# A turn's steps in another order: inverse, third norm and feed-forward part between the operator's product and the attention that uses it

## The chip, the cores and the metric

One core of a Trainium2 chip runs the whole program. The metric is the device time of one execution in microseconds (us), as the median of several runs. The core has five engines that each work through their own list of instructions in order: TensorE (PE, with its weight loads shown apart as PEld), VectorE (DVE), ScalarE (ACT), GpSimd (POOL) and SyncE (SP), which here only issues DMAs. They wait for each other by semaphores.

## What is computed

The input is 4 x 1024 rows of 256. A chunk is 128 rows, so there are 32 chunks, 8 to a batch. Cut to what matters:

```python
x = x + attn(layernorm(x))            # attn has a norm and a residual of its own
x = x + ffn(layernorm(x))             # "third norm"

def attn(x):                          # per head (16) and chunk (128 rows)
    G = K.T @ K + eps * I;  W = solve(G, K.T @ V)
    U = I[:, :8]
    for _ in range(2): U, _ = qr(W @ U)
    S = 0.9 * S + U @ (U.T @ W)       # state, carried from chunk to chunk of a batch
    out = 0.125 * (Q @ S)             # then @ Wo, + x

def ffn(x):                           # 256 -> 1024 -> 256, weights binarized
    h = gelu(x @ bw1.T + b1)
    return h @ bw2.T + b2
```

## The kernel before

Everything runs in float32, but for the feed-forward part, whose activations are split into a high and a low float16 half (`y3t`, `hsplit`). The first part of the program projects keys and values (L1286), forms the Gram products (L1332), inverts blocks of them by sweeps on DVE ("pivots", L1136, L1142, L1148), and works out low-rank factors per chunk, which go through DRAM (`f_d`). The queries are never formed: the factors of all heads of a chunk give one 256 x 256 operator.

The second part is 32 **turns**, one for each chunk. A turn has these steps:

- LF: SP loads the chunk's factors into `fl` (three buffers), after AU of three turns before was filled. LR: SP loads the residual rows, after the attention sum of two turns before.
- NB `apply_inverse` (PE, 8 matmuls, L1497), copied by ACT (L987) to `nb` (two buffers).
- AU `operator` (PE, 4 matmuls, L1504). DVE `decay` (L1204, L1201 on a batch's first chunk) adds it to 0.9 times the state before and writes one of two `state` buffers.
- AT `attend` (PE, 4 matmuls, L1511), which reads that state. DVE `attention_out` (L1213 to L1219) makes the residual sum `x2`, its statistics and the variance. POOL raises the variance to the power -1/2 (L781) and adds the output bias to `x2` (`biased`, L751).
- X3 `third_norm` (DVE, L1225) writes `x3`. Y3 `turn` (PE, 2 transpositions, L1519); ACT writes the high half of `y3t` (L993), DVE the low half (L1232).
- HID `hidden` (PE, 32 matmuls, L1531). GE0 and GE1, the two halves of `gelu` (ACT, 4 activations at L1002 and a cast at L1007 each). LO0 and LO1, `low` (POOL, L759), the low halves of the hidden values. LO1 waits for the cast of GE1.
- OUT `output` (PE, 16 matmuls, L1541), finished by DVE (L1238, L1241) and stored by SP.

The order is written by a planner, `plan()`, which runs on the host when the program is built. It has streams of steps (projections, Schur steps, solves, `tail`, and `turn`) and a simple clock for each engine with weights per step (`PE_WEIGHT`, `ACT_WEIGHT`, `DVE_WEIGHT`, `POOL_WEIGHT`). It takes the next step of a stream that can start, gives it a PSUM bank or two of the eight, and puts it into one list, `ORDER`. The stream `turn` comes last, so turns fill PE where the others can't. Within a stream the order is fixed. Every engine then walks through the same `ORDER` and does its own part of each step: `for step, c in ORDER:`. So the order of the steps of a turn is the order in PE's queue, in ACT's, in DVE's, in POOL's and in SP's. Two of these lists matter most here. POOL does its part of AT (L781, L751) and of LO0 and LO1 where these stand in the list; ACT does its part of Y3 (L993) and of GE0 and GE1 where these stand.

The tuple at L257 gives the order of a turn. Iteration r holds steps of several turns, r-2 to r+4. The pivots (step PIV) and the inverses of small blocks (SML) are put on DVE between the others, when the planner's clock of DVE says that it is free. POOL's MB (`block_small`, L742) spreads a batch's small inverses; for batches 2 and 3 it waits until the last NB of two batches before was filled.

Of the kernel before, what the change touches and what calls it, by code (L numbers as in the profile page):

```python
# [16 lines left out]
CPB = SEQ // CHUNK  # L17
# [23 lines left out]
             NB=1, AU=1, AT=1, Y3=1, HID=2, OUT=1)  # L41
# [1 line left out]
                 W=1.1, Y=.8, YT=.45, Z=.75, ZT=.5, BQ=1.87, BO=1.87, NB=.57, AU=.95, AT=.95, Y3=.35, HID=1.87, OUT=1.85)  # L43
ACT_WEIGHT = dict(T=.95, KL=.65, LG=.35, KC=.65, KT=.65, KA=.65, KB=.65, VA=.65, VB=.65, G=1.35, FT=1.1, FB=.4, QT=.65, SP=.65, SX=2.4, SV=.95, S=.45, U=2.1,
                  W=1.2, Y=.9, YT=1.0, Z=.45, ZT=.55, BQ=.65, BO=.65, NB=.45, Y3=.45, GE0=2.2, GE1=2.2)
DVE_WEIGHT = dict(AU=.75, AT=1.4, X3=.45, Y3=.5, OUT=.95)
POOL_WEIGHT = dict(LO0=1.25, LO1=1.25)

SMALL = ("SP", "SX", "SV", "S", "U", "W", "Y", "YT", "Z", "ZT", "NB", "Y3")
# [15 lines left out]
def pivot_weight(t):  # L65
    return .65 + .00204 * HALF * (HALF - 1 - t)


def plan():
# [4 lines left out]
    order, where, before = [], {}, {}  # L74
# [3 lines left out]
    now = dict(pe=0.0, act=0.0, dve=5.0, pool=5.0)  # L78
# [9 lines left out]
    def advance_dve():  # L88
        while True:
            while norms and now["dve"] <= now["pe"] + 4.0:  # L90
                g = norms[0]
                behind = FIRST[g] < sum(1 for c in range(NCH) if ("T", c) in where) + 4
                if staged and staged[0][1] <= now["dve"] + 1.0 and not behind:
                    break
                norms.pop(0)
                order.append(("LN", g))
                now["dve"] = max(now["dve"], now["pe"] - 2.0) + LN_WEIGHT * GROUPS[g] + .6
                for c in range(FIRST[g], FIRST[g] + GROUPS[g]):
                    at["LN", c] = now["dve"]
            for b, t in list(small_at.items()):  # L100
                if t <= now["pe"]:
                    del small_at[b]
                    order.append(("SML", b))
                    order.append(("MSTORE", b))
                    now["dve"] = max(now["dve"], t) + 8.0
                    spread_at[b] = now["dve"] + 3.0
            for b, t in list(spread_at.items()):
                if t <= now["pe"]:
                    del spread_at[b]
                    order.append(("MI", b))  # L110
                    mask_at[b] = now["pe"] + 4.0
            for b, t in list(mask_at.items()):
                if t <= now["pe"]:
                    del mask_at[b]
                    order.append(("MB", b))
                    small_done[b] = now["pe"] + 3.0
            ripe = [s for s in waiting if open_at.get(s, 1e9) <= now["pe"]]
            if ripe and len(staged) < 2:
                s = min(ripe, key=lambda s: s[1] + 1.5 * s[0])
                waiting.remove(s)  # L120
                sweep_order.append(s)
                j = len(sweep_order) - 1
                order.append(("SLOAD", j))
                staged.append((j, now["pe"] + 10.5))
                pivots[j] = 0
            if not staged:
                now["dve"] = max(now["dve"], now["pe"])
                return
            j, loaded = staged[0]
            start = max(now["dve"], loaded)  # L130
            if start > now["pe"] + DVE_BEHIND:
                return
            t = pivots[j]
            order.append(("PIV", (j, t)))
            now["dve"] = start + pivot_weight(t)
            pivots[j] += 1
            if pivots[j] == HALF:
                now["dve"] += .6
                order.append(("SSTORE", j))
                staged.pop(0)  # L140
                which, b = sweep_order[j]
                at["swept", which, b] = now["dve"] + 6.0
                if which == 0:
                    waiting.append((1, b))
# [31 lines left out]
    def put(step, c):  # L176
        order.append((step, c))
        if step in BANKS:
# [8 lines left out]
            if step in ACT_WEIGHT:  # L187
                now["act"] = max(now["act"], now["pe"] + .15) + ACT_WEIGHT[step]
                end = now["act"] + .15
                if step in DVE_WEIGHT:  # L190
                    now["dve"] = max(now["dve"], end) + DVE_WEIGHT[step]
                    end = now["dve"] + .15
            elif step == "HID":
                end = 1e9
            else:
                now["dve"] = max(now["dve"], now["pe"] + .15) + DVE_WEIGHT[step]
                end = now["dve"] + .15
# [8 lines left out]
        elif step == "X3":  # L206
            now["dve"] = max(now["dve"], at["AT", c] + 1.5) + DVE_WEIGHT[step]
            at[step, c] = now["dve"] + .1
# [11 lines left out]
        elif step == "BO" and c % half_batch == half_batch - 1:  # L220
            order.append(("MLOAD", c // half_batch))
            small_at[c // half_batch] = at["Z", c] + 7.0
        advance_dve()
        for b in small_done:
            at["small", b] = small_done[b]
# [28 lines left out]

    turn = []
    for r in range(-4, turns + 3):
        for step, n in (("LF", r + 4), ("LO1", r - 1), ("AT", r + 1), ("LR", r + 3), ("OUT", r - 2), ("X3", r + 1), ("NB", r + 2),  # L257
                        ("HID", r), ("GE0", r), ("AU", r + 2), ("LO0", r), ("Y3", r + 1), ("GE1", r)):
            if 0 <= n < turns:
                turn.append((step, n))  # L260

# [16 lines left out]
    def pause():  # L278
        now["pe"] += .25
        advance_dve()  # L280
        for b in small_done:
            at["small", b] = small_done[b]
# [17 lines left out]


ORDER, SWEEPS, WHERE, BEFORE = plan()


# [1323 lines left out]
```

## Time and profile before

| | us |
|---|---|
| median of 3 runs | 900.69 |
| lowest and highest | 897.38, 904.1 |
| the profiled execution | 900.93 |
| its span, first to last instruction | 899.1 |

| engine | busy us | share of the span |
|---|---|---|
| PE | 783.1 | 87% |
| PEld | 530.6 | 59% |
| DVE | 631.7 | 70% |
| ACT | 490.1 | 55% |
| POOL | 227.4 | 25% |

The profiled execution took 1.8 us more than its span. The rows of the trace below give the start of an instruction from the span's start, its duration, the engine and line, and in brackets how long the engine had been idle before it and what released it. Several instructions of one line in a row are merged into one row: its duration then runs from the first start to the last end.

### The profile page before, as it was taken

How to read it: one execution, taken by the hardware profiler on the slowest of the kernel's cores; microseconds unless marked ns; L12 is line 12 of the kernel's file. 1: busy time of each engine (PE TensorE's matmuls, PEld its weight loads, DVE VectorE, ACT ScalarE, POOL GpSimd, SP SyncE). 2: the span in 40 equal slices, each digit the busy share in tenths (PEclk: the TensorE clock that was granted, in tenths of full speed). 3: DMA queues.
4: the chain of work that ended last, by engine and by line, in shares of the span. 5: the costliest groups of instructions: out<-in, count | busy, mean ns of one | idle time of the engine just before them, and what ended most of it. 6: DMA issues, size and time to landing. Idle time of an engine off the chain costs nothing.

```text
span 899.1 us, 34359 instructions
## 1 busy us (share of the span) xinstructions
PE 783.1 (87%) x14730; PEld 530.6 (59%) x14730; DVE 631.7 (70%) x1336; ACT 490.1 (55%) x1068; POOL 227.4 (25%) x297
## 2 busy tenths in 40 slices
PE   4999999999999998988687687888798888899996
PEld 2555555565555555656455565666576666677775
DVE  3666399089998999980798988889953304666664
ACT  1864444555455454554444465556566665466665
POOL 4666100201001100000201012652012203555554
PEclk9999999999999999999879888999999999899999
DMA  8555211653455636655734645344456432222210
GB/s 313 155 159 167 77 62 42 205 177 122 139 162 160 185 72 168 185 162 168 162 79 119 188 116 159 103 135 116 107 154 138 104 93 69 62 82 74 77 43 30
DMA packets 174662, 114.43 MB, mean 127 GB/s; under 512 B 134128, under 2 KB 152944, under 8 KB 173488
## 3 DMA queue, kind: packets, MB, share of 16 engines
q1 hardware_dynamic: 168784, 91.00, 36.8%
q0 software_dynamic: 5728, 21.24, 7.5%
q8 instruction: 117, 1.92, 0.9%
q14 instruction: 33, 0.27, 0.1%
HBM read 61.22 MB, written 50.99 MB: 125 GB/s over the span
## 4 chain that ended last, share of the span: by engine, by line
PE 66%; DVE 13%; issue 9%; DMA 5%; ACT 4%; SPq 1%; POOL 1%; POOLq 0%; DVEq 0%; ACTq 0%
PE psum L1286 25%; PE psum L1332 6%; PE psum L1531 6%; PE psum L1541 5%; DVE outer L1142 4%; PE psum L1473 3%; PE psum L1511 3%; DVE work L1148 3%; PE psum L1504 2%; PE psum L1388 2%; PE psum L1375 2%; PE psum L1362 2%; PE psum L1423 2%; DVE state L1204 2%; PE psum L1497 1%
## 5 line engine op out<-in xcount | busy, mean ns | idle before, releaser
L1286 PE MATMUL psum<-wkv,xhat 128*128 128x512 f32 x512 | 240.3, 613 | 4.3 <-ACT xhat L834 4.3
L1142 DVE SCALAR_TENSOR_TENSOR outer<-work,rd 128x992 f32<-128x992 f32 (+30 forms) x248 | 189.6, 764 | 8.9 <-DVE rd L1136 0.3
L1148 DVE TENSOR_TENSOR work<-work,outer 128x992 f32<-128x992 f32 (+30 forms) x248 | 176.3, 711 | 8.6
L1286 PEld LDWEIGHTS psum<-wkv,xhat 128*128 128x128 f32 x512 | 93.2, 192 | 105.3 <-issue 99.5
L871 ACT COPY kv<-psum 128x512 f32<-128x512 f32 x128 | 75.1, 587 | 120.8 <-PE psum L1286 120.5
L1002 ACT ACTIVATE late<-psum,b1c,alpha 128x128 f32<-128x128 f32 x256 | 96.7, 461 | 49.6 <-PE psum L1531 49.6
L759 POOL TENSOR_TENSOR hsplit<-late,hsplit 128x512 f16<-128x512 f32 x64 | 77.4, 1211 | 142.4 <-ACT hsplit L1007 142.3
L1531 PEld LDWEIGHTS psum<-y3t,s1t 128*128 128x128 f16 x1024 | 61.3, 102 | 17.7 <-issue 16.7
L1531 PE MATMUL psum<-y3t,s1t 128*128 128x128 f16 x1024 | 66.9, 227 | 4.4 <-DVE y3t L1232 4.0
L1541 PE MATMUL psum<-s2t,hsplit 128*128 128x256 f16 x512 | 63.7, 279 | 4.0 <-POOL hsplit L759 2.7
L1332 PE MATMUL psum<-kv 128*64 128x128 f32 x1024 | 64.4, 280 | 0.0
L1541 PEld LDWEIGHTS psum<-s2t,hsplit 128*128 128x128 f16 x512 | 50.5, 100 | 15.6 <-issue 4.6
L1332 PEld LDWEIGHTS psum<-kv 128*64 128x64 f32 x1024 | 56.6, 139 | 4.9 <-issue 4.3
L1511 PE MATMUL psum<-state,xhat 128*128 128x256 f32 x128 | 39.4, 435 | 22.4 <-DVE state L1204 17.8
L1204 DVE SCALAR_TENSOR_TENSOR state<-state,psum 128x512 f32<-128x512 f32 x28 | 19.2, 686 | 42.3 <-PE psum L1504 42.3
L1133 DVE TENSOR_SCALAR work<-work 128x32 f32<-128x32 f32 x8 | 1.5, 192 | 65.7 <-DMA work<-lead_in_d 65.7
L1136 DVE RECIPROCAL rd<-work 128x1 f32<-128x1 f32 x256 | 41.7, 163 | 8.0
L1423 PE MATMUL psum<-cu,rr 64*64 64x64 f32 x1024 | 35.4, 230 | 8.9 <-issue 6.4
L1007 ACT CAST hsplit<-late 128x512 f16<-128x512 f32 x64 | 39.5, 618 | 5.9 <-ACT late L1002 0.7
L1511 PEld LDWEIGHTS psum<-state,xhat 128*128 128x128 f32 x128 | 24.2, 210 | 30.4 <-issue 25.0
L927 ACT COPY cu<-psum 32x1024 f32<-32x1024 f32 x32 | 32.1, 1005 | 17.5 <-PE psum L1410 17.3
L981 ACT COPY late<-psum 128x512 f32<-128x512 f32 x32 | 18.8, 586 | 40.4 <-PE psum L1473 40.0
(130 smaller groups left out, 1279.5 us busy)
## 6 DMA issues: line engine op xcount, KB each, us to landing
gc_d<-gc SPq DMA_DIRECT2D x32, 384.0 KB, 2.5
schur_mem<-gc_d SPq DMA_DIRECT2D x32, 384.0 KB, 4.2
f_d<-late SPq DMA_DIRECT2D x16, 512.0 KB, 3.6
late<-f_d SPq DMA_DIRECT2D x32, 256.0 KB, 2.7
sv_d<-sv SPq DMA_DIRECT2D x16, 384.0 KB, 3.1
lead_d<-work POOLq DMA_DIRECT2D x4, 1024.0 KB, 5.0
schur_mem<-lead_d SPq DMA_DIRECT2D x32, 128.0 KB, 4.3
r_d<-pt SPq DMA_DIRECT2D x16, 256.0 KB, 2.2
```

The costliest lines, as they stand in the source:

```text
L759: nc.gpsimd.tensor_tensor(hsplit[:, r % 2, 1, t].rearrange("p t r -> p (t r)"), ht[:, BANK * n:BANK * (n + 1)], hsplit[:, r % 2, 0, t].rea ...
L871: nc.scalar.copy(kv[:, n, BANK * half:BANK * (half + 1)], place(step, c)).then_inc(drain(step, c), 1)
L1002: nc.scalar.activation(ht[:, P * t:P * (t + 1)], place("HID", r)[:, P * t:P * (t + 1)], ACT.Gelu, scale=alpha1[:, t:t + 1], bias=b1c[:, t: ...
L1136: V.reciprocal(rd[:, t:t + 1], a[:, t, t:t + 1]).then_inc(swept, 1)
L1142: V.scalar_tensor_tensor(out=tile, in0=a[:, t, t + 1:HALF].unsqueeze(2).broadcast_to([P, m, HALF]), scalar=rd[:, t:t + 1], in1=a[:, t, t + ...
L1148: V.tensor_tensor(rest, rest, tile, ALU.subtract).then_inc(swept, 1)
L1286: ins = mm(dst[:], xnt[:, c, t], wkv[:, n, t, BANK * half:BANK * (half + 1)], start=t == 0, stop=t == KT - 1)
L1332: ins = mm(dst[side(a), P * h:P * (h + 1)], kv[:, 0, cols], kv[:, :, cols], start=True, stop=True)
L1423: ins = mm(dst[side(a ^ n), at:at + HD], u if turned else r, r if turned else u, start=True, stop=True)
L1511: ins = mm(dst[:, 0:DM], xnt[:, TURNS[r], t], state[:, r % 2, DM * t:DM * (t + 1)], start=t == 0, stop=t == KT - 1)
L1531: ins = mm(dst[:, P * t:P * (t + 1)], s1t[:, k, P * t:P * (t + 1)], y3t[:, part, k], start=k + part == 0, stop=k + part == KT)
L1541: ins = mm(dst[:, 0:DM], hsplit[:, r % 2, part, t], s2t[:, t], start=t + part == 0, stop=t + part == FT)
```

## The change

In `plan()` the steps of iteration r are put into another order, NB runs one turn further ahead, two weights of DVE are raised, and MB is placed only when the NB that it waits for stands in the list.

```diff
-DVE_WEIGHT = dict(AU=.75, AT=1.4, X3=.45, Y3=.5, OUT=.95)
+DVE_WEIGHT = dict(AU=.75, AT=1.4, X3=.8, Y3=.5, OUT=1.45)
...
             for b, t in list(mask_at.items()):
-                if t <= now["pe"]:
+                if t <= now["pe"] and (b < 2 or ("NB", CPB * (b - 1) - 1) in where):
                     del mask_at[b]
                     order.append(("MB", b))
...
     turn = []
     for r in range(-4, turns + 3):
-        for step, n in (("LF", r + 4), ("LO1", r - 1), ("AT", r + 1), ("LR", r + 3), ("OUT", r - 2), ("X3", r + 1), ("NB", r + 2),
-                        ("HID", r), ("GE0", r), ("AU", r + 2), ("LO0", r), ("Y3", r + 1), ("GE1", r)):
+        for step, n in (("LF", r + 4), ("LO1", r - 1), ("AT", r + 1), ("LR", r + 3), ("OUT", r - 2), ("AU", r + 2), ("NB", r + 3),
+                        ("X3", r + 1), ("HID", r), ("Y3", r + 1), ("GE0", r), ("LO0", r), ("GE1", r)):
             if 0 <= n < turns:
                 turn.append((step, n))
```

By engine, iteration r reads:

| engine | before | after |
|---|---|---|
| PE | AT(r+1) OUT(r-2) NB(r+2) HID(r) AU(r+2) Y3(r+1) | AT(r+1) OUT(r-2) AU(r+2) NB(r+3) HID(r) Y3(r+1) |
| DVE | AT(r+1) OUT(r-2) X3(r+1) AU(r+2) Y3(r+1) | AT(r+1) OUT(r-2) AU(r+2) X3(r+1) Y3(r+1) |
| ACT | NB(r+2) GE0(r) Y3(r+1) GE1(r) | NB(r+3) Y3(r+1) GE0(r) GE1(r) |
| POOL | LO1(r-1) AT(r+1) LO0(r) | LO1(r-1) AT(r+1) LO0(r) |
| SP | LF(r+4) LR(r+3) OUT(r-2) | LF(r+4) LR(r+3) OUT(r-2) |

The instructions themselves are the same in number and shape.

## Rows read from the trace of the kernel before

**Rows 1.** Busy time by stretch: bounds, length, engines, granted clock, DMA share, GB/s.

```profile
550.00:600.00 50.00, 40.49 (x532) 31.10 (x530) 41.20 (x97) 27.24 (x65) 27.62 (x33) 0.90 0.34 100
800.00:850.00 50.00, 45.44 (x465) 35.84 (x464) 31.70 (x64) 33.90 (x87) 25.90 (x28) 1.00 0.26 75
```

**Rows 2.** Groups by line: names, shapes, count; busy us, mean ns; idle before, releasers.

```profile
L1511 PE MATMUL psum<-state,xhat 128*128 128x256 f32 x128 | 39.4, 435 | 22.4 <-DVE state L1204 17.8 <-DVE state L1201 4.6
```

**Rows 3.** Timeline, PE alone, one turn of the last stretch.

```profile
822.28 1.10 PE L1511 MATMUL psum<-state,xhat 128*128 128x256 f32 x4 [0.65 <-DVE state L1204]
823.22 1.91 PE L1541 MATMUL psum<-s2t,hsplit 128*128 128x256 f16 x16
825.05 0.63 PE L1497 MATMUL psum<-late,mblock 32*32 32x256 f32 x8
825.62 1.96 PE L1531 MATMUL psum<-y3t,s1t 128*128 128x128 f16 x32
827.42 1.08 PE L1504 MATMUL psum<-late 128*128 128x256 f32 x4
828.34 0.38 PE L1519 MATMUL psum<-ident,x 128*128 128x128 f32 x2
829.38 1.10 PE L1511 MATMUL psum<-state,xhat 128*128 128x256 f32 x4 [0.66 <-DVE state L1201]
```

**Rows 4.** Timeline, the other engines in the same turn.

```profile
822.64 0.36 ACT L993 CAST y3t<-psum 128x256 f16<-128x256 f32 x1
...
822.91 1.51 ACT L1002 ACTIVATE late<-psum,b1c,alpha 128x128 f32<-128x128 f32 x4
...
825.20 1.16 POOL L759 TENSOR_TENSOR hsplit<-late,hsplit 128x512 f16<-128x512 f32 x1 [1.23 <-ACT hsplit L1007]
...
825.62 1.02 DVE L1241 TENSOR_TENSOR yo<-yo,x2b 128x256 f32<-128x256 f32 x1
...
826.32 0.73 POOL L781 TENSOR_TENSOR rs<-ve,half_neg 128x1 f32<-128x1 f32 x1
...
827.09 0.81 DVE L1225 TENSOR_SCALAR x<-x,mv,rs 128x256 f32<-128x256 f32 x1 [0.44 <-POOL rs L781]
...
828.54 0.69 DVE L1201 COPY state<-psum 128x512 f32<-128x512 f32 x1 [0.64 <-PE psum L1504]
```

**Rows 5.** Timeline, all engines, the last turns up to the end.

```profile
878.01 0.38 PE L1519 MATMUL psum<-ident,x 128*128 128x128 f32 x2
...
883.85 0.81 DVE L1225 TENSOR_SCALAR x<-x,mv,rs 128x256 f32<-128x256 f32 x1 [0.44 <-POOL rs L781]
...
884.80 0.41 PE L1519 MATMUL psum<-ident,x 128*128 128x128 f32 x2 [1.12 <-DVE x L1225]
...
888.80 1.51 ACT L1002 ACTIVATE late<-psum,b1c,alpha 128x128 f32<-128x128 f32 x4 [0.48 <-PE psum L1531]
...
890.92 1.50 ACT L1002 ACTIVATE late<-psum,b1c,alpha 128x128 f32<-128x128 f32 x4
...
893.20 1.15 POOL L759 TENSOR_TENSOR hsplit<-late,hsplit 128x512 f16<-128x512 f32 x1 [0.96 <-ACT hsplit L1007]
```

**Rows 6.** Timeline, three turns among pivots of DVE, and POOL's power there.

```profile
573.22 0.57 POOL L781 TENSOR_TENSOR rs<-ve,half_neg 128x1 f32<-128x1 f32 x1
...
584.74 1.10 PE L1511 MATMUL psum<-state,xhat 128*128 128x256 f32 x4 [1.69 <-DVE state L1204]
...
594.07 1.76 PE L1511 MATMUL psum<-state,xhat 128*128 128x256 f32 x4 [2.88 <-DVE state L1204]
...
602.84 1.10 PE L1511 MATMUL psum<-state,xhat 128*128 128x256 f32 x4 [0.66 <-DVE state L1201]
```

**Rows 7.** Timeline, two waits of PE outside these stretches.

```profile
488.95 2.05 PE L1511 MATMUL psum<-state,xhat 128*128 128x256 f32 x4 [2.80 <-DVE state L1201]
...
766.35 3.57 PE L1531 MATMUL psum<-y3t,s1t 128*128 128x128 f16 x32 [4.01 <-DVE y3t L1232]
```

**Rows 8.** DMA issues of the page: engine, count, KB each, us to landing.

```profile
late<-f_d SPq DMA_DIRECT2D x32, 256.0 KB, 2.7
```

## The prediction, as written before the changed kernel was run

> **What bounds the kernel now.** I read the busy times first, by stretch. In the last stretch, where nothing is left but turns, PE is busy 45.4 of 50 us at a granted clock of 1.00, and no other engine passes 36 [rows 1]. So a turn is worth what PE's queue takes for it, waits included. The groups by line then say where PE stands still in a turn: before AT it was idle for 22.4 us in all, and what ended that was DVE's `decay` [rows 2]. PE alone in one turn shows the pattern [rows 3]: from one AT to the next 7.10 us, of which 0.66 is that wait. The work is thus 6.44 us: by the starts AT 0.94, OUT 1.83, NB 0.57, HID 1.80, AU 0.92, Y3 0.38. The wait has its cause in the order: AU is followed by Y3 alone (0.38), while the decay that AT needs starts 1.12 after AU's start and takes 0.69 [rows 3, 4]. From 772.6 to 879.1 us sixteen ATs follow each other like this, 7.10 apart, all but one behind a wait of 0.64 to 0.66.
>
> **The change part by part.**
>
> *AU goes ahead of NB and HID.* Between AU(r+2) and the AT(r+2) that needs it now stand NB, HID and Y3: 0.57 + 1.80 + 0.38 = 2.75 us of PE's work, against 1.12 + 0.69 = 1.81 less AU's own 0.92. The wait before AT goes. Taken alone that is 0.66 of each turn, and 22.4 us of the span at the most [rows 2].
>
> *What comes late next.* The third norm needs POOL's power (L781), and POOL, in order, comes to it only after LO1(r-1), which stands ahead of AT(r+1) in the list. LO1(r-1) waits for the cast of GE1(r-1). That was so before. What is new is ACT's order: Y3(r) now stands ahead of both GE0(r-1) and GE1(r-1), before it stood between them. So each Y3 holds back the whole gelu of a turn, that gelu holds back LO1, LO1 the power, and the power the next Y3. This closes a ring from Y3 to the next Y3, and its length, worked out from rows:
>
> - Y3 start on PE to the high half on ACT: 0.42 (its own 0.38, and 0.04 as from AU's 827.42 + 1.08 to the decay at 828.54 [rows 3, 4]).
> - high half to GE0: 822.91 - 822.64 = 0.27 [rows 4].
> - GE0 to GE1: 890.92 - 888.80 = 2.12 [rows 5].
> - GE1 to LO1: 825.20 - 822.91 = 2.29 [rows 4].
> - LO1 to the power: 826.32 - 825.20 = 1.12 [rows 4].
> - the power to X3: 827.09 - 826.32 = 0.77 in this turn. The power took 0.73 there, beside DVE's `yo` sum of 1.02, and 0.57 in another turn [rows 4, 6]. With X3 waiting, nothing runs on DVE then, so I take 0.57 + 0.04 = 0.61.
> - X3 to Y3: 884.80 - 883.85 = 0.95 [rows 5].
>
> The sum is 7.78 us, or 7.94 with the slower power. In the order before, the ring ran from Y3 over GE1 alone: 7.78 - 2.12 = 5.66, shorter than the turn of 7.10, and PE never waited for it, except where it shows itself once: with AU and NB used up, the last Y3 came 1.12 late, behind X3 [rows 5].
>
> The Trainium skill, page "GPSIMD Engine Reference", section "1. Specifications", says that GpSimd's access to SBUF is shared with VectorE and contended by a DVE instruction with two SBUF inputs. The pair of 0.73 and 0.57 agrees. By it the ring would be 7.78 if the `yo` sum has ended by then, and 7.94 if not; it should have ended some 2 us before.
>
> A turn therefore costs max(6.44, 7.78) = 7.78, 0.68 more than before: the wait moves from AT (0.66) to Y3 (7.78 - 6.44 = 1.34).
>
> *How many turns.* From Y3(15) at about 771.5 to Y3(30) at 878.0 are 15 intervals, and one more to Y3(31): 16 x 0.68 = 10.9 us. Behind Y3(31) come 0.42 + 0.27 + 2.12 to GE1(30), 2.22 to GE0(31) (a gelu half with its cast: 822.91 plus 2.29, less the 0.07 to LO1), 2.12 to GE1(31), 2.29 to LO1(31), and then 899.12 - 893.20 = 5.92 to the end [rows 5], 15.36 in all. Before, the end came 899.12 - 878.01 = 21.11 after Y3(30) [rows 5]; now 7.78 + 15.36 = 23.14, so 2.0 more, of which 0.68 is counted. The sum is 10.9 + 1.3 = +12.2.
>
> *Turns among pivots.* Around 565 to 603 us PE has turns only, while DVE works on pivots. Their ATs waited up to 2.88, and the two intervals from 584.74 to 602.84 took 9.05 each, one of them with AT at 1.76 instead of 1.10, a spell at the lower clock behind the long wait [rows 6]. Bounds: if the waits go and nothing comes, the two turns fall to 7.78, 2.5 us less, and all five turns there lose some 3 to 5; if a pivot of over 2 us stands in front of X3, in the ring, they stay at 9 or pass it. I take -1.
>
> *Turns among other work.* There the turns are 12 to 48 us apart, the ring is no bound, and waits before AT go: 2.80 at 488.95 [rows 7], and four of 0.50 to 0.70. Against it stands that ACT, in order, now sits before Y3's high half with GE0 and every copy behind it. Bounds -5 and +3; I take -3. The 4.01 at 766.35 [rows 7], behind DVE's small inverse, I leave: HID waits for `y3t` in either order, only which turn it hits changes.
>
> *NB a turn further ahead.* It needs `fl` a turn earlier. The load lands 2.7 us after its issue [rows 8]; SP comes to it in iteration r-1 behind the store of OUT, and NB of that chunk is on PE in iteration r+1, so some 8 us of PE's work still cover it. If that cover were gone, 2.7 a turn at most. LF and LR stay where they were on SP, behind the same waits. The copy of NB on ACT (0.37) falls behind GE1 and has a turn until its AU. Nothing.
>
> *AU ahead of X3 on DVE.* The decay (0.69) ends 1.12 + 0.69 after AU's start, 0.38 + 0.94 + 1.83 + 1.81 = 4.96 us after the last Y3; X3 can start only 6.8 after it. Hidden, unless the ring were shorter than I say; then it is the next bound.
>
> *MB and the weights.* MB(2) and MB(3) already stand behind NB(7) and NB(15). Nothing. The larger weights move pivots a little; no more than the bounds above.
>
> Together 12.2 - 1 - 3 = +8.2: the profiled execution from 900.9 to 909.1, its span from 899.1 to 907.3. The median lies 0.2 under the profiled execution, so 908.9.
>
> **The rivals.**
>
> *The ring is hidden, the waits simply go* (faster). If the high half got to ACT without holding the gelu, or X3 were no longer behind LO1, each of 16 turns would fall to 6.44: -10.6, with the mixed part -4 to -8 more: 882 to 886. It decides the sign from a ring under 7.10. For it speaks only that PE has 0.66 to give back. Against it that each of the seven links has its row, and queues of ACT and POOL are in order.
>
> *The gains among other work are larger* (within 1%). The five waits there all go (-5), and the turns among pivots come down by 5 with the spell at the lower clock gone: 12.2 - 10 = +2.2, 903.
>
> *The mixed part loses too.* Pivots fall into the ring in five turns, at 1 to 2 us each, and Y3 waits now and then elsewhere: 12.2 + 5 to 10, 918 to 923.
>
> *PE's clock falls in the last stretch.* Now a wait of 1.34 us stands in each turn. A wait of 1.69 was followed by an AT of 1.10, at full clock, one of 2.88 by 1.76 [rows 6], and HID behind 4.01 took 3.57 instead of 1.96 [rows 3, 7]. So 1.34 should keep the 2.4 GHz. At 1.2 GHz, by the ratios 1.76/1.10 and 3.57/1.96, 6.44 would be some 11 us: if a fifth of the last sixteen turns went so, 3 x 3.2 = +10, 919. The Trainium skill, page "TensorE: Matmul & The Clock Gate", section "A second HAM failure mode: psum-queue depth-cycling", tells of a kernel whose frequent small pauses between groups of matmuls make the clock swing; the granted 1.00 over waits of 0.65 in each turn [rows 1, 3] does not bear that out here, and no row has 1.34 in each turn.
>
> **How the numbers follow.** The forecast's case (905 to 913) 0.46, larger gains 0.22, losses in the mixed part 0.15, the clock 0.08, the hidden ring 0.09. The range leaves out the hidden ring and the far end of the losses: 899 to 920. About 1% is what a measurement of this kernel can tell from no change; that is 891.7 to 909.7. Faster has the hidden ring, 0.08. The forecast's case lies on the upper edge: a little over half of it, with the larger gains, is within 1%, so 0.48; the rest is slower, 0.44.
>
> **What would show it.** In the changed kernel's last stretch: Y3 to Y3 at 7.8 us, no wait before L1511, one of 1.3 before L1519 released by DVE's `x` (L1225), X3 released by POOL's power, the power straight behind L759, L993 just ahead of L1002. Wrong if Y3 has no wait there, if the turn is 6.5, or if 7.8 holds and the total still falls: then the mixed part gave back more than 12.

## The result, and the profile after

| | before | after |
|---|---|---|
| median, us | 899.04 (4 runs) | 921.91 (4 runs) |
| lowest to highest | 893.63 to 904.1 | 916.88 to 927.04 |
| profiled execution, its span | 900.93, 899.1 | 916.88, 915.0 |

The ratio is 1.0256 (95% interval 1.0162 to 1.035). Six more runs on another chip, beside new ones of before, give 1.027 (1.0194 to 1.0345). The change makes the kernel some 2.6% slower. I had forecast 908.9 (899 to 920), 8.2 us more than before, and it is 22.9: the right side, much too small, and outside the range. The profiled execution, 916.88, is the fastest of the four.

PE does the same work in less of a longer span. Its waits by group of instructions (busy us, mean ns, idle before):

```profile
L1511 PE MATMUL psum<-state,xhat 128*128 128x256 f32 x128 | 36.0, 407 | 0.0
L1519 PE MATMUL psum<-ident,x 128*128 128x128 f32 x64 | 14.1, 305 | 44.2 <-DVE x L1225 44.1
L1531 PE MATMUL psum<-y3t,s1t 128*128 128x128 f16 x1024 | 64.5, 222 | 10.2 <-DVE y3t L1232 9.3 <-issue 0.6 <-ACT hsplit L1007 0.3
```

The 22.4 us before AT [rows 2] are gone to the last tenth, and 44.2 stand before Y3, where there were 1.4. The kernel before:

```profile
L1519 PE MATMUL psum<-ident,x 128*128 128x128 f32 x64 | 13.0, 287 | 1.4 <-DVE x L1225 1.1 <-ACT wmem L936 0.2
```

One turn of the last stretch of the changed kernel, all engines, in order of time:

```profile
803.36 1.16 POOL L759 TENSOR_TENSOR hsplit<-late,hsplit 128x512 f16<-128x512 f32 x1 [0.96 <-ACT hsplit L1007]
804.48 0.55 POOL L781 TENSOR_TENSOR rs<-ve,half_neg 128x1 f32<-128x1 f32 x1
...
805.07 0.80 DVE L1225 TENSOR_SCALAR x<-x,mv,rs 128x256 f32<-128x256 f32 x1 [1.78 <-POOL rs L781]
806.01 0.41 PE L1519 MATMUL psum<-ident,x 128*128 128x128 f32 x2 [1.43 <-DVE x L1225]
806.26 1.03 PE L1511 MATMUL psum<-state,xhat 128*128 128x256 f32 x4
806.46 0.37 ACT L993 CAST y3t<-psum 128x256 f16<-128x256 f32 x1 [2.90 <-PE psum L1519]
806.73 1.51 ACT L1002 ACTIVATE late<-psum,b1c,alpha 128x128 f32<-128x128 f32 x4
...
808.86 1.50 ACT L1002 ACTIVATE late<-psum,b1c,alpha 128x128 f32<-128x128 f32 x4
...
811.14 1.16 POOL L759 TENSOR_TENSOR hsplit<-late,hsplit 128x512 f16<-128x512 f32 x1 [0.96 <-ACT hsplit L1007]
812.25 0.55 POOL L781 TENSOR_TENSOR rs<-ve,half_neg 128x1 f32<-128x1 f32 x1
...
812.84 0.81 DVE L1225 TENSOR_SCALAR x<-x,mv,rs 128x256 f32<-128x256 f32 x1 [1.78 <-POOL rs L781]
813.79 0.41 PE L1519 MATMUL psum<-ident,x 128*128 128x128 f32 x2 [1.43 <-DVE x L1225]
```

This is the ring as the prediction has it. From Y3 at 806.01: 0.45 to the high half, 0.27 to GE0, 2.13 to GE1, 2.28 to LO1, 1.11 to the power, 0.59 to X3, 0.95 to the next Y3 at 813.79. The sum is 7.78 us. PE waits 1.43 in each turn, for X3; X3 waits for the power.

The busy times by stretch, with the granted clock as the third number from the end, are:

```profile
550.00:600.00 50.00, 35.81 (x858) 28.28 (x858) 38.06 (x78) 26.68 (x60) 22.36 (x25) 0.83 0.49 108
800.00:850.00 50.00, 41.42 (x433) 32.68 (x431) 28.93 (x60) 31.39 (x81) 22.20 (x25) 1.00 0.23 67
```

Against [rows 1] PE has lost 4.7 and 4.0 us of 50; the clock is 0.83 instead of 0.90 in the first and still 1.00 in the second, with a wait of 1.43 in every turn. The first stretch holds other steps in the two kernels (858 matmuls here, 532 before), so that only the second compares like with like. The long waits of PE in the first part all have DVE's queue behind them:

```profile
549.25 0.17 DVE L1164 RECIPROCAL mrd<-msw 128x1 f32<-128x1 f32 x1 [8.21 <-DMA msw<-m_d]
...
556.35 0.41 DVE L1232 TENSOR_TENSOR y3t<-psum,y3t 128x256 f16<-128x256 f32 x1
...
556.91 3.57 PE L1531 MATMUL psum<-y3t,s1t 128*128 128x128 f16 x32 [9.29 <-DVE y3t L1232]
...
570.21 0.20 DVE L1133 TENSOR_SCALAR work<-work 128x32 f32<-128x32 f32 x1 [4.37 <-DMA work<-sv_d]
...
573.04 0.41 DVE L1225 TENSOR_SCALAR x<-x,mv,rs 128x256 f32<-128x256 f32 x1
...
573.59 0.66 PE L1519 MATMUL psum<-ident,x 128*128 128x128 f32 x2 [4.97 <-DVE x L1225]
...
735.63 0.66 PE L1519 MATMUL psum<-ident,x 128*128 128x128 f32 x2 [7.55 <-DVE x L1225]
```

At 549 DVE, in order, sits 8.2 us on a load for the inverse of small blocks (SML), with the low half of Y3(0) behind it, and HID(0) waits 9.29; the HID then takes 3.57 instead of 1.96, and the granted clock from 556 to 561 us is 0.50. At 570 it is a sweep's load and first pivot ahead of X3. At 735 it is SML again, whose small operations hold DVE from 724.3 to 733.8.

**Where the 15.9 us of the two profiled executions lie.** In the changed kernel the other work ends at about 720, with Y3(9) at 721.8; before, at 755, with Y3(14) at 757.9. So five turns fewer had been done by then, and five more stand in the last stretch. Before, Y3(14) to Y3(31) took 884.8 - 757.9 = 126.9; after, Y3(9) to Y3(31) took 899.5 - 721.8 = 177.7, less five turns of 7.10 is 142.2: +15.3. The end behind Y3(31) is 15.5 instead of 14.3: +1.2. What is left, -0.6, is the part among other work. This is a sum for two single executions: that of before was 2 us over its median, that of after 5 under.

### The profile page after: what moved, and what is told of

Same layout as the page of the kernel before. It is cut to its first block, busy times and chain, and to the rows that moved or that the text cites. A ratio compares the mean times of both kernels' runs of the same rounds, so it can differ in the third digit from the quotient of the medians.

```text
span 915.0 us, 34354 instructions
## 1 busy us (share of the span) xinstructions
PE 781.8 (85%) x14730; PEld 529.7 (58%) x14730; DVE 627.2 (69%) x1336; ACT 487.5 (53%) x1068; POOL 225.6 (25%) x297
## 4 chain that ended last, share of the span: by engine, by line
PE 45%; DVE 22%; issue 9%; ACT 9%; POOL 7%; DMA 5%; SPq 2%; POOLq 0%; ACTq 0%; DVEq 0%
PE psum L1286 24%; DVE outer L1142 8%; DVE work L1148 6%; PE psum L1332 6%; POOL hsplit L759 5%; ACT late L1002 4%; DVE x L1225 2%; PE psum L1473 2%; PE psum L1388 2%; DVE rd L1136 2%; ACT hsplit L1007 2%; PE psum L1375 2%; PE psum L1362 2%; PE psum L1423 1%; POOL rs L781 1%
## 5 line engine op out<-in xcount | busy, mean ns | idle before, releaser
L1142 DVE SCALAR_TENSOR_TENSOR outer<-work,rd 128x992 f32<-128x992 f32 (+30 forms) x248 | 186.8, 753 | 8.9 <-DVE rd L1136 0.3
L1148 DVE TENSOR_TENSOR work<-work,outer 128x992 f32<-128x992 f32 (+30 forms) x248 | 172.9, 697 | 8.5
L759 POOL TENSOR_TENSOR hsplit<-late,hsplit 128x512 f16<-128x512 f32 x64 | 75.0, 1172 | 156.6 <-ACT hsplit L1007 156.5
L1002 ACT ACTIVATE late<-psum,b1c,alpha 128x128 f32<-128x128 f32 x256 | 96.5, 460 | 0.0
L1531 PE MATMUL psum<-y3t,s1t 128*128 128x128 f16 x1024 | 64.5, 222 | 10.2 <-DVE y3t L1232 9.3
L1531 PEld LDWEIGHTS psum<-y3t,s1t 128*128 128x128 f16 x1024 | 59.1, 99 | 22.7 <-issue 11.5
L993 ACT CAST y3t<-psum 128x256 f16<-128x256 f32 x32 | 12.0, 374 | 90.0 <-PE psum L1519 89.9
L1232 DVE TENSOR_TENSOR y3t<-psum,y3t 128x256 f16<-128x256 f32 x32 | 13.6, 423 | 63.0 <-ACT y3t L993 63.0
L1519 PE MATMUL psum<-ident,x 128*128 128x128 f32 x64 | 14.1, 305 | 44.2 <-DVE x L1225 44.1
L1225 DVE TENSOR_SCALAR x<-x,mv,rs 128x256 f32<-128x256 f32 x32 | 23.4, 731 | 37.0 <-POOL rs L781 36.9
```

The costliest lines, as they stand in the source:

```text
L759: nc.gpsimd.tensor_tensor(hsplit[:, r % 2, 1, t].rearrange("p t r -> p (t r)"), ht[:, BANK * n:BANK * (n + 1)], hsplit[:, r % 2, 0, t].rea ...
L1002: nc.scalar.activation(ht[:, P * t:P * (t + 1)], place("HID", r)[:, P * t:P * (t + 1)], ACT.Gelu, scale=alpha1[:, t:t + 1], bias=b1c[:, t: ...
L1142: V.scalar_tensor_tensor(out=tile, in0=a[:, t, t + 1:HALF].unsqueeze(2).broadcast_to([P, m, HALF]), scalar=rd[:, t:t + 1], in1=a[:, t, t + ...
L1148: V.tensor_tensor(rest, rest, tile, ALU.subtract).then_inc(swept, 1)
L1531: ins = mm(dst[:, P * t:P * (t + 1)], s1t[:, k, P * t:P * (t + 1)], y3t[:, part, k], start=k + part == 0, stop=k + part == KT)
```

## The experiments

Each ran beside the kernel before. Ratios are to it, with their 95% intervals; "turn" is the time from turn to turn in the last stretch of the profile. Letters are those of the sections below.

| run | what | ratio | turn, us |
|---|---|---|---|
| changed, again | (A) | 1.027 (1.019 to 1.035) | 7.78 |
| gelu_first | (B) GE0 ahead of Y3 | 1.0108 (1.006 to 1.0157) | 6.97 |
| power_first | (B) power ahead of LO1 | 0.9872 (0.9828 to 0.9917) | 6.16 |
| power_only | (B) the same on the old order | 1.0049 (1.0014 to 1.0083) | 7.10 |
| bias_first | (B) ring lengthened | 1.0316 (1.025 to 1.0381) | 8.05 |
| old_then_new | (C) | 1.0108 (1.0055 to 1.0162) | 7.78 |
| new_then_old | (C) | 1.0100 (1.0066 to 1.0134) | 7.10 |
| old_then_power | (C) | 0.9897 (0.9853 to 0.9942) | 6.16 |
| power_from_4 | (C) | 0.9861 (0.9771 to 0.995) | 6.16 |
| weights_only | (D) | 1.0162 (1.011 to 1.0214) | 7.10 |
| old_weights | (D) | 1.0387 (1.0322 to 1.0452) | 7.78 |
| old_weights_power | (D) | 1.0008 (0.9966 to 1.005) | 6.16 |
| small_later | (E) | 1.0291 (1.0246 to 1.0336) | 7.78 |
| small3_later | (E) | 1.023 (1.0173 to 1.0287) | 7.78 |
| small3_power | (E) | 0.9845 (0.9786 to 0.9904) | 6.16 |

**(A) The changed kernel again.**

> The changed kernel once more, beside the next three on one chip, for a narrower interval: 1.020 to 1.030 of before by either theory, the turns of the last stretch at 7.78.

It held: 1.027, 7.78.

**(B) Is it the ring?** Two cuts, at different links:

```diff
 gelu_first:   ... ("X3", r + 1), ("HID", r),
-              ("Y3", r + 1), ("GE0", r), ("LO0", r), ("GE1", r)
+              ("GE0", r), ("LO0", r), ("Y3", r + 1), ("GE1", r)
 power_first:  ("LF", r + 4),
-              ("LO1", r - 1), ("AT", r + 1),
+              ("AT", r + 1), ("LO1", r - 1),
```

> The changed kernel, but with LO1(r-1) behind AT(r+1) in the list, so that POOL does the power and the bias sum of AT before LO1; ACT's order stays that of the change. Theory of the ring: LO1 is no longer in front of the power, the ring is cut at this link, and a turn of the last stretch takes 6.4 to 6.5 us, as with the gelu half moved: span about 886. If ACT's wait for Y3's transposition were itself the price, the turn would stay above 7 us here.

It held for the turn, and went further: 6.16, the span 879.9. That is 19 under the span of before in its one profile, but against the median of before beside this run (895.13, with 885.93 for this kernel) it is only 9 us. Some 20 turns shorter by 0.94 would be 19, so about 10 are lost elsewhere by the medians. PE, POOL and DVE in the last stretch:

```profile
799.69 1.03 PE L1504 MATMUL psum<-late 128*128 128x256 f32 x4
...
800.95 0.73 POOL L781 TENSOR_TENSOR rs<-ve,half_neg 128x1 f32<-128x1 f32 x1
...
801.79 0.73 DVE L1225 TENSOR_SCALAR x<-x,mv,rs 128x256 f32<-128x256 f32 x1
802.34 1.20 POOL L759 TENSOR_TENSOR hsplit<-late,hsplit 128x512 f16<-128x512 f32 x1
803.01 0.39 PE L1519 MATMUL psum<-ident,x 128*128 128x128 f32 x2
803.24 1.03 PE L1511 MATMUL psum<-state,xhat 128*128 128x256 f32 x4
...
804.10 1.91 PE L1541 MATMUL psum<-s2t,hsplit 128*128 128x256 f16 x16
...
805.85 1.03 PE L1504 MATMUL psum<-late 128*128 128x256 f32 x4
```

The power comes before LO1, X3 ends at 802.5, and Y3 at 803.01 has no wait; AU to AU is 6.16. So a turn's work on PE is 6.16 and not the 6.44 that I took as 7.10 less the wait of 0.66. Start to start, 0.81 of the 0.94 lie between Y3 and AT (1.04 before, 0.23 here, for a recorded wait of 0.65), and 0.08 between AT and OUT (0.94 before, 0.86 here). The last 0.05 have nothing to do with the wait: OUT takes 1.83 to 1.84 with NB behind it and 1.75 with AU behind it, and AU takes 0.03 more with NB behind it than with Y3. The rows of the old order in weights_only, at a place with no wait before AT, show the 1.84 all the same:

```profile
784.87 1.03 PE L1511 MATMUL psum<-state,xhat 128*128 128x256 f32 x4
785.74 1.91 PE L1541 MATMUL psum<-s2t,hsplit 128*128 128x256 f16 x16
787.58 0.63 PE L1497 MATMUL psum<-late,mblock 32*32 32x256 f32 x8
```

The wait before AT, recorded as 0.65, had thus cost 0.89 a turn.

> The changed kernel, but with GE0 and LO0 of iteration r put back ahead of Y3(r+1) (as before the change). Theory of the ring: the ring from one Y3 to the next is then 7.78 - 2.12 = 5.66 us, under PE's 6.44 of work, and AU still stands well ahead of AT. So in the last stretch no wait is left before L1511 or L1519, a turn takes 6.4 to 6.5 us, and with some 22 turns there the span falls by 22 x 1.3 = 29 us from 915 to about 886, which is also below the 899 of before. Theory of the planner (the loss comes from where the steps fall among the other work, not from the ring): turns stay near 7.8 or find a new wait, and the span stays above 905.

A miss, in the turn and in the total. The wait of each turn is gone, but one in every second turn has come, and the turns are 6.6 and 7.4 long. The span is 903.0 where 886 was expected, and the ratio 1.0108, though its turns are shorter than the 7.10 of before. The last stretch gives back some 22 x 0.13 = 2.9 us and the end costs 2.0, and the medians are 10 apart, so about 11 us are lost in front of it: in the total the theory of the planner came nearer. PE alone:

```profile
818.08 0.41 PE L1519 MATMUL psum<-ident,x 128*128 128x128 f32 x2 [1.04 <-DVE x L1225]
...
822.57 1.96 PE L1531 MATMUL psum<-y3t,s1t 128*128 128x128 f16 x32
...
824.64 0.41 PE L1519 MATMUL psum<-ident,x 128*128 128x128 f32 x2
...
832.02 0.41 PE L1519 MATMUL psum<-ident,x 128*128 128x128 f32 x2 [1.04 <-DVE x L1225]
```

Two turns take 13.94. There is a second ring, through two turns, which my sum had left out. In the trace of this run it goes from HID(r) at 822.57 to GE0(r) 2.00, to the high half of Y3(r+1) 2.11, to GE1(r) 0.27, to LO1(r) 2.29, to the power 1.25, to X3 0.58, and to Y3(r+2) at 832.02 0.95. From a Y3 that waited (818.08) PE's Y3, AT, OUT, AU and NB take 0.28 + 0.94 + 1.74 + 0.96 + 0.57 = 4.49 to HID. The sum is 13.94, 6.97 a turn, with no slack in it. That this ring sets the pace was not tried by cutting it. If it does, then with POOL's and ACT's old order the hoisted AU could give 7.10 - 6.97 = 0.13 a turn at the most.

```diff
 bias_first, at POOL's part of AT:
+                    biased(c)
                     pool.wait_ge(ve3_ready, c + 1)
                     nc.gpsimd.tensor_tensor(rs3[:], ve3[:], half_neg[:, 0:1], ALU.pow)...
-                    biased(c)
```

> The changed kernel with POOL's two operations of AT swapped: the bias sum (0.72 us) ahead of the power. Theory of the ring: the bias sum comes into the ring (+0.72), and X3, no longer beside it, falls from 0.81 to 0.41 (-0.40): a turn of the last stretch goes from 7.78 to 8.10 us, 22 turns make +7 us against the changed kernel, ratio to before about 1.033. If the wait before Y3 had another cause, the turn stays at 7.78.

It held: 8.05 us for 8.10, and X3 at 0.41 with nothing beside it on POOL. All engines:

```profile
815.95 0.72 POOL L751 TENSOR_TENSOR x2b<-x,b2r 128x256 f32<-128x256 f32 x1
816.63 0.55 POOL L782 TENSOR_TENSOR rs<-ve,half_neg 128x1 f32<-128x1 f32 x1
817.21 0.41 DVE L1225 TENSOR_SCALAR x<-x,mv,rs 128x256 f32<-128x256 f32 x1 [2.46 <-POOL rs L782]
...
817.77 0.41 PE L1519 MATMUL psum<-ident,x 128*128 128x128 f32 x2 [1.71 <-DVE x L1225]
...
825.83 0.41 PE L1519 MATMUL psum<-ident,x 128*128 128x128 f32 x2 [1.71 <-DVE x L1225]
```

`power_only` puts `("AT", r + 1)` ahead of `("LO1", r - 1)` in the kernel before and changes nothing else:

> The kernel before, with one step moved: LO1(r-1) behind AT(r+1), so that POOL does the power ahead of LO1; AU stays where it was. Theory: before the change the power was not late, PE waited for the state; a turn stays at 7.10 and the time does not change (ratio 0.995 to 1.005). If POOL's order were the whole gain of the kernel with LO1 moved, it would show here: a turn near 6.5, ratio below 0.99.

It held: alone, POOL's order gives nothing; by the interval it costs 0.1 to 0.8%. It is worth something only with the wait for the state gone, and of the kernels tried here that hoist AU only those with this swap are faster than before.

**(C) The last stretch and the rest apart.** The turn tuple by iteration, old order and new order joined at a seam (in words; the tuples themselves are those shown above):

```diff
 old_then_new:    old order (old weights) for r < 16, then the changed one; one extra NB at r = 16
 new_then_old:    changed order for r < 11, then the old one, changed weights throughout; NB left out at r = 11
 old_then_power:  as old_then_new, with AT ahead of LO1 from r = 16
 power_from_4:    the same from r = 4
```

> The order of before up to iteration 15, the changed order from iteration 16 on (one extra NB at the seam); the DVE weights of before. The part of the program among other work is that of before, only the last stretch is changed. Theory of the ring: some 15 turns at 7.78 instead of 7.10 and 1.3 at the end, +11 to +12: span 911. Theory of the planner: about 899, no change.

> The changed order and weights up to iteration 10, the order of before from iteration 11 on. Only the part among other work is changed. Theory of the ring: some 20 turns at 7.10 instead of 7.78 and the end of before, so 915 - 14 - 1.3 = about 899.5, level with before. Theory of the planner: the loss of 16 stays, about 912 to 915.

The first held (+1.08%, 9.7 us, with 11 to 12 expected): the ring, in the 14 turns that have it there. The second did not: the last stretch is back at 7.10, and yet 1.0% (9 us) stay. In its profile the seam costs about 3 of them (three turns there take 24.3 instead of 21.3); so some 6 us, 3 to 9 by the interval, are lost among the other work, to order and weights together. The profiled pair above had shown none (-0.6), for the reason given there. The ring and the rest are both needed for the 2.6%.

> The order and weights of before up to iteration 15; from iteration 16 on the changed order, but with LO1(r-1) behind AT(r+1). The kernel with LO1 moved in all turns ran 1.3% under the one of before; its turn took 6.17 us in the last stretch, 0.93 under the 7.10 of before. Theory (the changed order costs some 6 us among the other work, besides the ring): here that part is the old one, so 15 turns x 0.93 = 14 us less than before, ratio about 0.984, below the 0.987 of the other. If the part among other work costs nothing, the other kernel should stay ahead, since it has some 20 turns at 6.17.

> The weights of before; the old order of a turn up to iteration 3 and the changed one with LO1 behind AT from iteration 4 on. The planner puts 15 transpositions Y3 ahead of the last output factors, as many as before. If the old start is what kept that part cheap, and the cut ring gives 0.93 in each turn of the last stretch and a part of it earlier: 16 x 0.93 = 15 us, ratio 0.978 to 0.985. If the part among other work costs the same in either order: 0.987 to 0.990, as the two kernels with a cut ring before.

The first missed: 0.9897, not 0.984, and no better than power_first. The turns do take 6.16, and its profiled span is 884.5, 14.6 under that of before; the medians give 10. The other 4 are the distance of the one profiled execution of before (900.93) from the median beside this run (896.32); whether that is chance I can't say. The second, 0.9861, lies between the ranges of its two cases, and its interval reaches into both.

**(D) The weights of DVE.** Only the line `DVE_WEIGHT` is changed, in weights_only together with the condition on MB. On the old order that condition changes nothing: `plan()` writes the same list with it and without it, so weights_only shows the weights alone.

```diff
 weights_only, on the old order:
-DVE_WEIGHT = dict(AU=.75, AT=1.4, X3=.45, Y3=.5, OUT=.95)
+DVE_WEIGHT = dict(AU=.75, AT=1.4, X3=.8, Y3=.5, OUT=1.45)
 old_weights, and old_weights_power with AT ahead of LO1, on the changed order:
-DVE_WEIGHT = dict(AU=.75, AT=1.4, X3=.8, Y3=.5, OUT=1.45)
+DVE_WEIGHT = dict(AU=.75, AT=1.4, X3=.45, Y3=.5, OUT=.95)
```

> The kernel before, with the changed DVE weights and the changed condition on MB, but the old order of a turn. The planner then puts 17 instead of 14 transpositions Y3 ahead of the last output factors. Theory: the weights alone are not the loss; a turn of the last stretch stays 7.10, and the time is within 1% of before. If the loss among other work came from the weights, about +6 us here.

> The changed order with the DVE weights of before. The weights alone, on the old order, cost 1.6% (14 us). Theory A (the loss among other work in the changed kernel comes from the weights): the ring stays, turns at 7.78, but the rest comes back: ratio 1.010 to 1.018. Theory B (with the changed order the planner's choice is poor with either weights; it puts 10 transpositions Y3 ahead of the last output factors here, 9 in the changed kernel, 14 before): ratio 1.020 to 1.030, as the changed kernel.

> The changed order with LO1 behind AT (which ran at 0.987 of before) and the DVE weights of before. Theory A: the weights' part comes back on top, 0.972 to 0.980. Theory B: 0.985 to 0.990, no gain by the weights.

The theory of the first fell: the weights alone cost 1.6% on the old order. Theory A of the others fell too, the other way: with the old weights the changed order is worse still, 1.0387, and with the ring cut 1.0008 instead of 0.9872. The new weights harm the old order and help the new one, by 1.2 to 1.6% each. They change nothing but the planner's list: where pivots and inverses stand among the turns, and how many turns come before the last stretch (17 Y3 ahead of the last output factors in weights_only, 14 before). More turns placed early did not make it faster. Two stretches of weights_only, the first PE alone, the second with SML3 on DVE from 790.42 to 797.6, ahead of the decay:

```profile
571.74 0.66 PE L1519 MATMUL psum<-ident,x 128*128 128x128 f32 x2 [4.09 <-DVE x L1225]
...
574.36 2.05 PE L1511 MATMUL psum<-state,xhat 128*128 128x256 f32 x4 [1.96 <-DVE state L1204]
...
790.42 0.15 DVE L1164 RECIPROCAL mrd<-msw 128x1 f32<-128x1 f32 x1
...
798.33 2.05 PE L1511 MATMUL psum<-state,xhat 128*128 128x256 f32 x4 [7.08 <-DVE state L1204]
```

and in old_weights, DVE and PE:

```profile
741.73 0.17 DVE L1164 RECIPROCAL mrd<-msw 128x1 f32<-128x1 f32 x1 [5.67 <-DMA msw<-m_d]
...
749.41 0.49 DVE L1225 TENSOR_SCALAR x<-x,mv,rs 128x256 f32<-128x256 f32 x1
...
750.05 0.66 PE L1519 MATMUL psum<-ident,x 128*128 128x128 f32 x2 [12.01 <-DVE x L1225]
```

Here SML3 stands in front of the decay and X3, waits 5.67 for its load first, and PE waits 12.01 before Y3, against 7.55 in the changed kernel. With the changed order the weights of before are thus no repair.

**(E) The inverses of small blocks.** `small_at` is where the planner thinks an inverse can start (in words; it is `at["Z", c] + 7.0` for all batches in the changed kernel):

```diff
 small_later:                 at["Z", c] + (16.0 for batch 1, else 7.0)
 small3_later, small3_power:  at["Z", c] + (11.0 for batch 3, else 7.0)
```

> The changed kernel with batch 1's inverse of small blocks (SML1) put on DVE some 9 us later by the planner's clock: behind HID(0) in the list instead of ahead of the low half of Y3(0). Theory: PE's wait of 9.29 before HID(0) came from this inverse, which DVE, in order, held for 8.2 us on a load; it goes, and 3 to 9 us of the span with it, unless the next turn's Y3 waits in its place. The last stretch stays at 7.78. Rival (the place of the inverse is hidden by something else late there): no change.

The wait of 9.29 did go, and within the intervals nothing came back: 1.0291, against 1.027 with it. In this run HID(0) follows at 548.77 with no wait, but other waits stand behind it:

```profile
557.58 1.93 PE L1410 MATMUL psum<-vv,st 32*32 32x64 f32 x64 [2.38 <-ACT st L918]
...
567.30 0.66 PE L1519 MATMUL psum<-ident,x 128*128 128x128 f32 x2 [4.42 <-DVE x L1225]
```

So this wait was the largest of the profile, and yet moving it gave back nothing that these runs can tell.

> The changed kernel with batch 3's inverse of small blocks (SML3) some 4 us later by the planner's clock: behind X3(10) and HID(9) instead of ahead of AU(11) and X3(10). Theory: the wait of 7.55 before Y3(10) goes, since X3 is no longer behind 9 us of DVE's small operations; the gelu runs meanwhile, and a wait of about 4 before HID(10) comes for it, as before the change. 3 to 4 us less than the changed kernel, ratio to before 1.021 to 1.024. Rival: it costs the same wherever it stands, 1.026.

> The kernel with LO1 behind AT in all turns (0.987 of before), with SML3 moved as well. Theory: 3 to 4 us less than that kernel, 0.983. Rival: 0.987.

Both came out as the theory has it (1.023, 0.9845), but the intervals reach to the rival. The profile is plainer: in small3_later the 7.55 before Y3(10) is gone, 2.96 before HID(10) has come, and Y3(9) to Y3(11) takes 742.7 - 723.1 = 19.6 instead of 743.7 - 721.8 = 21.9.

```profile
737.72 0.41 DVE L1232 TENSOR_TENSOR y3t<-psum,y3t 128x256 f16<-128x256 f32 x1
...
738.28 3.45 PE L1531 MATMUL psum<-y3t,s1t 128*128 128x128 f16 x32 [2.96 <-DVE y3t L1232]
```

small3_power has the lowest ratio found: 1.6% under the kernel before and some 4% under the changed one. By the intervals it can't be told from power_first or power_from_4.

## Why the prediction was wrong in size

Two steps of the prediction failed: the number of turns at the ring's pace, and the part among pivots and other work, with the weights that I priced at nothing. The ring itself was right.

*What bounds the kernel before* was right, but for the price: the wait before AT cost 0.89 a turn, not 0.66.

*The ring* was right link by link: 7.78 forecast, 7.78 measured, with the power at 0.55 as taken, and cutting or lengthening a link moved the turn as it should in power_first and bias_first. X3 was released by the power, L993 stood ahead of L1002, no wait was left before L1511: all as listed. One reading behind it was too simple. The 0.57 that I set against the 0.73 was no power without the `yo` sum: the sum ran there too, but began 0.13 after the power. The 0.55 in each turn of the changed kernel, with DVE idle, bears out the value all the same.

*How many turns* was the first step that failed, a term mis-sized. I carried over the 16 of the trace of before. The planner, with the changed order and weights, had placed five turns fewer when the other work ended, and 21 to 22 run at the pace of the ring: +15.3 instead of +10.9. This could not be read from the trace, but it was not hidden: `plan()` runs on the host, and its list has 14 Y3 ahead of the last output factors before the change and 9 after.

*The end*: +1.3 forecast, +1.2 measured.

*Turns among pivots and among other work* was the second: -4 forecast, and nothing gained. The profiled pair shows -0.6, new_then_old some +6. The waits before AT went as said (none is left), but the sequence of DVE that the planner then wrote put SML and first pivots ahead of Y3's low half and X3. I had named a pivot in front of X3 as the upper bound for the five turns among pivots, and for SML wrote that "only which turn it hits changes": the wait changed from 4.01 to 9.29 and 7.55. (The two intervals given as 9.05 each took 9.33 and 8.77; 9.05 is their mean.)

*MB and the weights* belongs to the same step, and there it failed in kind: "they move pivots a little; no more than the bounds above". On the old order the weights alone are +1.6%, some 14 us against an upper bound of +3, and on the changed order the same weights are worth some 1.2% the other way.

*NB a turn further ahead* and *AU ahead of X3* were set at nothing and not tried by themselves. In the changed kernel no wait stands before AU, and none before NB in the last stretch.

*The rival that came true* is "the mixed part loses too", 918 to 923, which I gave 0.15; 921.91 lies in it. Its reason, pivots and waits in front of Y3, is what the profiles show, but its number is in part luck: it took +12.2 from the last stretch and 5 to 10 from the rest, and the runs give 15.3 + 1.2 and some 6. I gave most, 0.48, to a change within 1%.

*The clock* held at 1.00 in the last stretch, over waits of 1.43, and that rival fell. From 480 to 600 us it was 0.79, against 0.89 before; from 600 to 700 us 0.98, against 0.95. Over all the profiles the first of these stretches has 0.76 to 0.83 in the kernels that start with the changed order and 0.83 to 0.90 in those that start with the old one. That this is a cause of its own, and not just what follows the longer waits, was not tested.

*The hidden ring* fell. That the ring of the old order had slack (5.66) was true of the ring of one turn alone. The way through two turns was there as well: without AU in it, but with the wait for the state (1.04 + 0.94 + 1.83 + 0.57 = 4.38 from Y3 to HID), and the other links as in gelu_first and rows 3 to 5, it took 13.90 of the 14.20 of two turns.

What stays open is the split of the loss among the other work. The weights shift it by 1.2 to 1.6%, up on one order and down on the other, and taking away single long waits gave nothing once and perhaps 0.3% once. I take it for what a list laid out by rough clocks does with engines that keep order; no run shows that.

## What to carry to other kernels

When a step is hoisted to hide a wait, follow every queue in which its neighbours moved, and add up the rings through several engines, over one turn and over two: in the changed kernel no engine but PE was over 69% busy, and the pace was set by a ring of ACT, POOL, DVE and PE that a single swap (Y3 ahead of GE0 on ACT) had closed. The cure was one swap elsewhere (POOL's power ahead of LO1), which alone is worth nothing, and with the hoist brings the kernel from 2.7% over the one before to 1.3% under it. Where a planner writes the order, a changed weight is a change to the whole schedule, and its effect is to be measured apart from that of the order it comes with. Where the planner runs on the host, compare its two lists first: here the five turns fewer and the new places of SML stood in them.

## What the hardware showed that was not expected

- A wait of PE costs more than its record: with nothing to wait for AT starts 0.23 after Y3's start, and behind a recorded wait of 0.65 it starts 1.04 after. AT to OUT is then 0.94 instead of 0.86. The recorded 0.65 cost 0.89.
- What a group costs depends on the one behind it: OUT takes 1.83 to 1.84 with NB behind it (8 matmuls of 32 x 32 tiles) and 1.75 with AU, whether PE waited before or not.
- The granted clock stayed at the 2.4 GHz level through the whole last stretch with a wait of 1.43 us (changed) and of 1.71 us (bias_first) in every turn of 8 us. Behind a wait of 7.55 the transposition took 0.66 instead of 0.41, behind one of 9.29 HID took 3.57 instead of 1.96. The Trainium skill (page "TensorE: Matmul & The Clock Gate", section "A second HAM failure mode: psum-queue depth-cycling") tells of short pauses that make the clock swing; no run here shows that at 1.4 to 1.7 us a turn.
- The third norm (L1225) takes 0.41 us with POOL idle, 0.80 beside POOL's bias sum, and 0.73 in power_first, where LO1 follows at its end. The power takes 0.55 with DVE idle and 0.73 when the `yo` sum is already running at its start; where the sum begins after the power (573.22 and five more in the profile before) the power takes 0.55 to 0.57. The Trainium skill (page "GPSIMD Engine Reference", section "1. Specifications") says that GpSimd shares its access to SBUF with VectorE and is contended by VectorE instructions with two SBUF inputs or in a 2-port mode. The power's rows agree, since the `yo` sum has two such inputs. The third norm has one input tensor, and no run shows whether it is in such a mode.
